# New engine orders, padded memory products and discarded products in a fused attention and dynamic-convolution kernel

## The chip, the cores and the metric

One NeuronCore of a Trainium2 chip runs the kernel. The metric is the device time in microseconds. Five instruction streams run side by side: TensorE (PE), VectorE (DVE), ScalarE (ACT), GpSimd (POOL) and SyncE (SP), which here only issues DMAs. Each executes its own list in order; they meet through semaphores.

## What is computed

The input is 16 images of 128 channels and 32 x 32 pixels, in float32. Two stages follow each other, each on a group norm of its input and each added to it.

```
x = x + attention(group_norm(x))       # linear attention, 4 heads of 32, 4 memory keys and values
x = x + dynamic_conv(group_norm(x))    # 3 x 3 convolution, filters mixed per image from 3 experts

# attention: q is normalised over the channels of a head, k over all pixels
xn = rmsnorm(x) * g1
q, k, v = w_qkv @ xn                    # k and v get 4 memory columns more
q = softmax(q, over channels) * scale;  k = softmax(k, over pixels)
context = k @ v.T;  out = context.T @ q
out = rmsnorm(w_out @ out + b_out) * g2

# dynamic convolution: a gate per expert and input channel, from 16 pooled cells
y = relu(rconv_w @ pooled(x) + rconv_b);  r = sigmoid(relu(fc_w @ y + fc_b))
w = sum over experts k of r[k, c] * expert_weight[k, o, c, :, :]
out = conv3x3(x, w)                     # padding 1
```

## The kernel before

One image has its channels on the 128 partitions and its 1024 pixels along the row. Eight tiles of 128 pixels each are turned on TensorE where pixels have to stand on the partitions.

The work is a software pipeline over images. In step `t` each engine works on several images at once: a part that is called with age `a` works on image `t - a`. `do(part, t, p, a)` issues a part for that image if there is one, `turn` does the same for the shared group statistics (of image `t` for the first norm and `t - 3` for the second), and `once` puts a part of the setup into one step. Steps run from -1 to 20. Those up to 8 and from 15 on are written out (unrolled), and those from 9 to 14 are three rounds of a loop of two steps. Nothing reorders the instructions: each engine has its own function `step(t, p)`, and the order of the lines in it is the order of its list.

The main parts, by engine and with the line of the profile:

- TensorE. The transposes of x (L1122) feed the sum of squares. Each of the eight `project` tiles has three products of rounded operands (L1135 to L1137). The transpose of the partial key maximum (L1143) and its spread over all partitions (`k_shift`, L1148) give the key maximum. `key_contexts` has one product with the 4 memory keys (L1154) and eight with the tiles (L1156). Then come the transposes of its result (L1161) and of q (`q_transpose`, L1179), `contexts` with the 4 memory values (L1166) and the rest (L1167), `mixes` (L1171), `outputs` (L1189) and the transposes of y (L1195). The group norms need two small products, the group means (L1110) and the group variances (L1115). `routing` (L1202) feeds the gates. The convolution has 54 products an image (L1225), 27 for each half of the image; `conv(n)` issues the next n of them, so they fill the list between the other parts. A plain float32 product is run as two passes, which the profile counts as two instructions. The convolution and the projections use operands split into a rounded part and a rest, in one pass a product.
- VectorE. The maxima over keys and queries, the subtractions and sums of the softmaxes, the statistics, the second residual (L900), the gates, the passes over the filters (L999, L1006, and L1012, which adds one to the centre tap), and the low part of the image (L936). `rms1` (L785) scales the eight sums of squares of an image; GpSimd raises them to the power -1/2 (L490).
- ScalarE. The exponentials, the squares, the high parts (`high1` L582, `filters_high` L659), the first pass over the filters (`w_first`, L653, which writes into the space of expert_raw), and the evacuations of PSUM (the projections' is L592, the result's L668).
- GpSimd. The low parts of x and of the filters (L483, L528), the scaling of q_exp (`q_normalise`, L501) and of x_nt (L495), the first norm (L476), the powers, and four small operations that zero the edge columns of the shifted images (`image_edges`, L535).
- SyncE. The loads of an image twice (`xa`, `xb`), the store, and four copies of the image shifted by one pixel.

The experts' filters are turned in nine groups of TensorE transposes during steps 0 to 2 (`expert_transpose`, L1094), through the PSUM buffers `ps_conv` of the convolution; ScalarE (L674) and VectorE (L989) evacuate them. The first convolution runs in step 4.

The memory tiles `memk_exp`, `memv_t` and `mem_ones` have 4 partitions, so the products L1154 and L1166 use 4 rows of the array:

```
mm(ps_att[:, 0:CEXT], memk_exp[:, :], mem_ones[:, :], start=True, stop=False)
mm(ps_att[:, 0:HID], memv_t[:, :], memk_exp[:, :], start=True, stop=False)
```

## Time and profile before

| | |
|---|---|
| median of 3 runs | 477.28 us (476.15 to 477.4) |
| the profiled execution | 476.64 us, span 474.9 us |
| TensorE busy, mean granted clock | 425.4 us (90%), 0.96 |
| VectorE busy | 373.1 us (79%) |
| ScalarE busy | 293.3 us (62%) |
| GpSimd busy | 253.3 us (53%) |
| HBM | 58 GB/s over the span |

The span is counted from the first to the last instruction. Busy time is the time in which at least one instruction of an engine runs. Matmuls are pipelined, so that a busy TensorE is not one at its peak: the distance from one start to the next says more than a duration does. A chain of waits is followed back from the last instruction, at each step to what released it; "issue" in it is time in which the engine waited for nothing that the profile shows.

### The profile page before, as it was taken

The numbers are of one execution on the slowest core, as the hardware profiler recorded it, in microseconds if no ns is written. First come the engines' busy times: TensorE is split into PE (matmuls) and PEld (weight loads), VectorE is DVE, ScalarE is ACT, GpSimd is POOL, SyncE is SP. The second block draws the span as 40 slices with busy tenths as digits, with TensorE's granted clock in tenths as the row PEclk, the third lists the DMA queues.
The fourth block names the chain that finished last, engine by engine and source line by source line (L and its number), as shares of the span: only waits on it lengthen the run. The fifth ranks groups of instructions, "written<-read, shape, count | busy, mean of one in ns | idle before, by whom it ended". The sixth has DMA issues, their size and how long they took to land.

```text
span 474.9 us, 8615 instructions
## 1 busy us (share of the span) xinstructions
PE 425.4 (90%) x2478; PEld 357.6 (75%) x2478; DVE 373.1 (79%) x773; ACT 293.3 (62%) x903; POOL 253.3 (53%) x247
## 2 busy tenths in 40 slices
PE   2868775999999999999999999999999999999796
PEld 1757674888778787878787787878788877868575
DVE  3374969798998979797979989797979797886720
ACT  2575676566676776766666667767666667554221
POOL 4635554648283747556482837575564838242220
PEclk9969595999999999999999999999999999999899
DMA  7320224224434160626243341605252332424331
GB/s 215 129 89 2 88 90 177 91 88 149 162 129 183 58 238 16 224 88 224 88 160 152 121 188 53 239 17 221 88 221 89 124 143 89 178 77 190 134 132 44
DMA packets 18786, 61.61 MB, mean 130 GB/s; under 512 B 2992, under 2 KB 4032, under 8 KB 18752
## 3 DMA queue, kind: packets, MB, share of 16 engines
q1 hardware_dynamic: 18752, 61.21, 34.1%
q8 instruction: 15, 0.25, 0.2%
q14 instruction: 19, 0.16, 0.1%
HBM read 19.29 MB, written 8.39 MB: 58 GB/s over the span
## 4 chain that ended last, share of the span: by engine, by line
PE 33%; DVE 31%; issue 23%; ACT 6%; DMA 3%; SPq 1%; DVEq 1%; POOL 1%; POOLq 0%; ACTq 0%
PE ps_conv L1225 7%; PE ps_y L1189 6%; DVE w_full L1006 4%; DVE stats L907 3%; DVE q_sum L848 3%; PE ps_y L1179 3%; DVE route_terms L954 3%; ACT expert_raw L653 3%; DVE k_half L792 2%; PE ps_att L1156 2%; DMA expert_raw<-_conv_expert_weight_dram 2%; DVE y_scaled L888 2%; ACT qk L592 2%; DVE x L900 2%; PE ps_qkv L1135 2%
## 5 line engine op out<-in xcount | busy, mean ns | idle before, releaser
L592 ACT ACTIVATE qk<-ps_qkv,scale 128x256 f32<-128x256 f32 x128 | 55.0, 468 | 13.8 <-PE ps_qkv L1137 13.8
L659 ACT ACTIVATE w_hi<-w_full 128x1152 fp32r<-128x1152 f32 x16 | 18.7, 1167 | 60.6 <-DVE w_full L1012 60.6
L528 POOL TENSOR_TENSOR w_lo<-w_full,w_hi 128x1152 fp32r<-128x1152 f32 x16 | 42.6, 2662 | 23.7 <-ACT w_hi L659 13.6
L509 POOL TENSOR_TENSOR scale<-ssq,minus_half 128x8 f32<-128x8 f32 x16 | 26.2, 1637 | 44.3 <-DVE ssq L881 44.3
L1135 PE MATMUL ps_qkv<-wqk_hi,x_hi 128*128 128x256 f32 x128 | 42.4, 331 | 3.7 <-ACT qk L592 3.7
L483 POOL TENSOR_TENSOR x_lo<-x,x_hi 128x1024 fp32r<-128x1024 f32 x16 | 38.2, 2387 | 12.8 <-ACT x_hi L582 12.8
L535 POOL TENSOR_TENSOR left_hi<-zeros 128x32 fp32r<-128x32 f32 x16 | 4.0, 250 | 75.0 <-DMA right_lo<-img_lo 75.0
L633 ACT ACTIVATE y_scaled<-ps_y 128x128 f32<-128x128 f32 x128 | 33.3, 291 | 12.7 <-PE ps_y L1189 12.7
L1225 PE MATMUL ps_conv<-left_hi,w_lo 128*128 128x512 f32 (+1 forms) x96 | 39.8, 414 | 0.0
L1225 PE MATMUL ps_conv<-img_hi,w_lo 128*128 128x512 f32 x96 | 39.7, 413 | 0.0
L1225 PE MATMUL ps_conv<-img_hi,w_hi 128*128 128x512 f32 x96 | 38.5, 401 | 1.1 <-POOL w_lo L528 1.1
L1225 PE MATMUL ps_conv<-right_lo,w_hi 128*128 128x512 f32 (+1 forms) x96 | 39.1, 408 | 0.0
L1225 PE MATMUL ps_conv<-right_hi,w_hi 128*128 128x512 f32 (+1 forms) x96 | 38.7, 403 | 0.0
L1225 PE MATMUL ps_conv<-img_lo,w_hi 128*128 128x512 f32 x96 | 38.5, 401 | 0.0
L1225 PE MATMUL ps_conv<-left_hi,w_hi 128*128 128x512 f32 (+1 forms) x96 | 37.8, 394 | 0.0
L1225 PE MATMUL ps_conv<-left_lo,w_hi 128*128 128x512 f32 (+1 forms) x96 | 37.8, 393 | 0.0
L1225 PE MATMUL ps_conv<-right_hi,w_lo 128*128 128x512 f32 (+1 forms) x96 | 37.6, 392 | 0.0
L1136 PE MATMUL ps_qkv<-wqk_lo,x_hi 128*128 128x256 f32 x128 | 36.9, 288 | 0.0
L1137 PE MATMUL ps_qkv<-wqk_hi,x_lo 128*128 128x256 f32 x128 | 36.8, 288 | 0.0
L1156 PE MATMUL ps_att<-x_nt,k_exp 128*128 128x130 f32 x256 | 36.1, 298 | 0.0
L1156 PEld LDWEIGHTS ps_att<-x_nt,k_exp 128*128 128x128 f32 x256 | 32.9, 207 | 2.2 <-issue 0.5
L565 ACT ACTIVATE squares<-ps_qkv 128x128 f32<-128x128 f32 x128 | 33.1, 275 | 1.5 <-PE ps_qkv L1122 1.5
(147 smaller groups left out, 1327.7 us busy)
## 6 DMA issues: line engine op xcount, KB each, us to landing
xa<-in_x_dram SPq DMA_DIRECT2D x16, 512.0 KB, 4.0
xb<-in_x_dram SPq DMA_DIRECT2D x16, 512.0 KB, 4.8
out_dram<-expert_raw SPq DMA_DIRECT2D x16, 512.0 KB, 2.9
left_hi<-img_hi SPq DMA_DIRECT2D x16, 511.5 KB, 2.9
right_hi<-img_hi SPq DMA_DIRECT2D x16, 511.5 KB, 3.7
left_lo<-img_lo SPq DMA_DIRECT2D x16, 511.5 KB, 2.9
right_lo<-img_lo SPq DMA_DIRECT2D x16, 511.5 KB, 3.7
expert_raw<-_conv_expert_weight_dram SPq DMA_DIRECT2D x1, 1728.0 KB, 8.6
```

Of the source, the lines that this page charges most:

```text
L483: nc.gpsimd.tensor_tensor(x1_lo[:, :], x1[:, :], x1_hi[:, :].bitcast(F32), ALU.subtract).then_inc(x1_lo_done, 1)
L509: nc.gpsimd.tensor_tensor(scale2[:, :], ssq2[:, :], minus_half[:, :], ALU.pow).then_inc(scale2_done, 1)
L528: nc.gpsimd.tensor_tensor(w_lo[p][:, :, :].rearrange("p t o -> p (t o)"), w_full[:, :], w_hi[p][:, :, :].bitcast(F32).rearrange("p t o -> ...
L565: last = nc.scalar.activation(squares[:, tile(t)], ps_qkv[h][:, tile(t % (NT // 2))], ACT.Square, accum_out=ssq1_sum[:, t:t + 1])
L592: nc.scalar.activation(qk[:, t, :], ps_qkv[t % 2][:, 0:QK], ACT.Copy, scale=scale1[:, t:t + 1]).then_inc(qkv_done, 1)
L633: last = nc.scalar.activation(y_scaled[:, t, :], ps_y[:, tile(t)], ACT.Square, accum_out=ssq2_sum[:, t:t + 1])
L1135: mm(o, x1_hi[:, tile(t)], wqk_hi[:, :], start=True, stop=False)
L1136: mm(o, x1_hi[:, tile(t)], wqk_lo[:, :], start=False, stop=False)
L1137: mm(o, x1_lo[:, tile(t)], wqk_hi[:, :], start=False, stop=True).then_inc(qkv_ps, 1)
L1156: last = mm(ps_att[:, 0:CEXT], k_exp[:, t, :], x_nt[p][:, t, :], start=False, stop=(t == NT - 1))
L1189: last = mm(ps_y[:, tile(t)], q_t[p][:, tile(t)], mix[p][:, :], start=True, stop=True)
L1225: last = mm(into, weight[:, tap, :], pixels[:, top + down:bottom + down, :], start=(n == 0), stop=(n == 3 * TAPS - 1))
```

## The change

It has three parts.

**Orders.** The order of the lines in `step` of TensorE, VectorE and ScalarE is new. GpSimd's list keeps its cyclic order and is only cut into steps at another place; SyncE's is the same. Ages that grow by one mean the same: on ScalarE and VectorE, too, the cut between two steps moves, and parts ahead of it are called with an age larger by one.

**Padding.** `memk_exp`, `memv_t` and `mem_ones` have 128 partitions. GpSimd sets the first two to zero at the start, and only their first 4 partitions are written afterwards, so that L1154 and L1166 have 128 rows and give the same sums.

**Discarded products.** `keep_busy` issues products of a tile of ones, 64 columns wide, into an unused part of `ps_stat`, at five places of steps 2 and 3 alone. Their results are never read.

```
-        memv_t = sb("memv_t", [MEM, HID])
-        mem_ones = sb("mem_ones", [MEM, CEXT])
+        memv_t = sb("memv_t", [128, HID])
+        mem_ones = sb("mem_ones", [128, CEXT])
-        memk_exp = sb("memk_exp", [MEM, HID])
+        memk_exp = sb("memk_exp", [128, HID])
+            nc.gpsimd.memset(memv_t[:, :], 0.0)
+            nc.gpsimd.memset(memk_exp[:, :], 0.0)
...
-                nc.scalar.activation(memk_exp[:, :], memk_exp[:, :], ACT.Exp).then_inc(memk_exp_done, 1)
+                nc.scalar.activation(memk_exp[0:MEM, :], memk_exp[0:MEM, :], ACT.Exp).then_inc(memk_exp_done, 1)
...
+            IDLE_PRODUCTS = {"key_contexts": {2: 8, 3: 6}, "project": {2: 6, 3: 6}, "k_part_transpose": {2: 5, 3: 9},
+                             "k_shift": {2: 4, 3: 4}, "y_transpose": {2: 2, 3: 3}}
+
+            def keep_busy(t, place):
+
+                if not isinstance(t, int) or t not in IDLE_PRODUCTS[place]:
+                    return
+                turns = t if place == "key_contexts" else t + 1
+                pe.wait_ge(gvar_done, turns)
+                if turns > GAP:
+                    pe.wait_ge(route_y_done, turns - GAP)
+                for _ in range(IDLE_PRODUCTS[place][t]):
+                    mm(ps_stat[:, 448:512], ones[:, :], ones[:, 0:64], start=True, stop=True)
...
+                once(expert_transpose, t, 0, 0)
+                do(x_transpose, t, p, 0, 0)
+                do(x_transpose, t, p, 0, 1)
+                keep_busy(t, "k_part_transpose")
                 do(k_part_transpose, t, p, 1)
...
                 do(y_transpose, t, p, 2)
-                conv(2)
-                once(expert_transpose, t, 0, 0)
+                conv(1)
```

The last piece also shows two moves of the first steps: the first group of expert transposes, which waits for the load of the experts, stands ahead of the transposes of the first image, where it stood behind them; and both halves of the transposes of x stand ahead of the transpose of the partial key maximum. The other eight expert groups, spread over steps 1 and 2, are spread over steps 1 to 3.

On ScalarE, `high1` (L582) moves from ahead of `filters_high` to behind the exponential of q, and the first half's result from behind `filters_high` to ahead of it.

VectorE, in a middle step, from the last pass over the gates to the residual of y (gate_n are the gates, k_max_part and k_max_all the partial and the full key maximum). Before:

```order
L936 SCALAR_TENSOR_TENSOR img_lo<-x_1,nmean,img_hi 128x1024
L999 SCALAR_TENSOR_TENSOR w_second<-experts,gate_n,expert_raw 128x1152
L792 TENSOR_TENSOR k_half<-qk 128x512
L798 TENSOR_TENSOR k_quarter<-k_half 128x256
L804 TENSOR_TENSOR k_max_part<-k_quarter 128x128
L1006 SCALAR_TENSOR_TENSOR w_full<-experts,gate_n,w_second 128x1152
L833 TENSOR_REDUCE q_max<-qk 128x32
L1012 TENSOR_TENSOR w_full<-w_full,ident 128x128
L811 TENSOR_REDUCE k_max<-ps_att 128x1
L840 TENSOR_TENSOR q_exp<-qk,q_max 128x1024
L818 TENSOR_SCALAR k_max_all<-k_max,memk_max 128x1
```

After (the lines of the changed kernel are a few higher):

```order
L938 SCALAR_TENSOR_TENSOR img_lo<-x_0,nmean,img_hi 128x1024
L748 BN_AGGR meanvar<-stats 128x2
L1001 SCALAR_TENSOR_TENSOR w_second<-experts,gate_n,expert_raw 128x1152
L794 TENSOR_TENSOR k_half<-qk 128x512
L1008 SCALAR_TENSOR_TENSOR w_full<-experts,gate_n,w_second 128x1152
L835 TENSOR_REDUCE q_max<-qk 128x32
L800 TENSOR_TENSOR k_quarter<-k_half 128x256
L1014 TENSOR_TENSOR w_full<-w_full,ident 128x128
L806 TENSOR_TENSOR k_max_part<-k_quarter 128x128
L842 TENSOR_TENSOR q_exp<-qk,q_max 128x1024
L813 TENSOR_REDUCE k_max<-ps_att 128x1
L820 TENSOR_SCALAR k_max_all<-k_max,memk_max 128x1
```

The partial maximum has moved behind the centre tap's addition, the full one with it, and the aggregate of the first norm has come in.

VectorE, the stretch that follows, from the sums of q to the group means (nmean). Before:

```order
L848 TENSOR_REDUCE q_sum<-q_exp 128x32
L854 RECIPROCAL q_rsum<-q_sum 128x32
L900 SCALAR_TENSOR_TENSOR x_1<-ps_y,g_c,xb 128x1024
L785 TENSOR_SCALAR ssq<-ssq_sum 128x8
L907 BN_STATS stats<-x_1 128x6 x2
L746 BN_AGGR meanvar<-stats 128x2
L915 BN_AGGR meanvar<-stats 128x2
L921 TENSOR_REDUCE pooled<-x_1 128x16
L757 TENSOR_SCALAR nmean<-ps_stat 128x2
```

After:

```order
L850 TENSOR_REDUCE q_sum<-q_exp 128x32
L856 RECIPROCAL q_rsum<-q_sum 128x32
L902 SCALAR_TENSOR_TENSOR x_1<-ps_y,g_c,xb 128x1024
L909 BN_STATS stats<-x_1 128x6 x2
L787 TENSOR_SCALAR ssq<-ssq_sum 128x8
L917 BN_AGGR meanvar<-stats 128x2
L923 TENSOR_REDUCE pooled<-x_1 128x16
L759 TENSOR_SCALAR nmean<-ps_stat 128x2
```

The scaling of the sums of squares (L785, now L787) has moved behind the statistics, and the first norm's aggregate is gone from here.

TensorE, from the key contexts to the contexts. Before:

```order
L1154 MATMUL ps_att<-mem_ones,memk_exp 128x130
L1156 MATMUL ps_att<-x_nt,k_exp 128x130 x8
L1225 MATMUL ps_conv<-left_hi,w_lo 128x480
...
L1225 MATMUL ps_conv<-img_hi,w_hi 128x480
L1225 MATMUL ps_conv<-img_lo,w_hi 128x480
L1110 MATMUL ps_stat<-meanvar,group_avg 128x2
L1161 MATMUL ps_att<-ident,k_x 128x128
L1179 MATMUL ps_y<-ident,q_exp 128x128 x8
L1166 MATMUL ps_att<-memk_exp,memv_t 128x128
```

After:

```order
L1156 MATMUL ps_att<-mem_ones,memk_exp 128x130
L1158 MATMUL ps_att<-x_nt,k_exp 128x130 x8
...
L1241 MATMUL ps_conv<-img_hi,w_hi 128x480
L1241 MATMUL ps_conv<-img_lo,w_hi 128x480
L1181 MATMUL ps_y<-ident,q_exp 128x128 x4
L1163 MATMUL ps_att<-ident,k_x 128x128
L1112 MATMUL ps_stat<-meanvar,group_avg 128x2
L1181 MATMUL ps_y<-ident,q_exp 128x128 x4
L1168 MATMUL ps_att<-memk_exp,memv_t 128x128
```

The group means (L1110, now L1112) have moved behind half of the transposes of q and the transpose of k_x.

## Rows read from the trace of the kernel before

**Rows 1.** The page: TensorE's granted clock in 40 slices of 11.9 us, in tenths.

```profile
PEclk9969595999999999999999999999999999999899
```

**Rows 2.** Busy time by stage: length, busy us and count per engine, PEclk, DMA.

```profile
34.00:56.00 22.00, 16.73 (x99) 14.94 (x98) 13.96 (x27) 13.76 (x54) 11.40 (x8) 0.73 0.15 54
56.00:79.00 23.00, 14.79 (x87) 13.37 (x87) 18.61 (x42) 14.12 (x41) 11.52 (x13) 0.72 0.36 138
131.00:157.00 26.00, 24.82 (x154) 21.00 (x153) 23.17 (x49) 18.04 (x57) 15.60 (x15) 1.00 0.38 143
```

**Rows 3.** The chain of waits, whole run: start us, us, what (passes).

```profile
56.41 3.77 PE ps_att L1156 x16
...
73.95 1.41 DVE w_full L1006
...
142.64 1.78 PE ps_y L1189 x16
...
212.61 2.00 PE ps_att L1156 x16
...
412.28 1.41 DVE w_full L1006
...
439.02 0.89 PE ps_y L1195 x8
...
458.51 12.52 PE ps_conv L1225 x54
```

**Rows 4.** VectorE's timeline, one step: start, us, instruction, [idle before, releaser].

```profile
125.80 1.41 DVE L1006 SCALAR_TENSOR_TENSOR w_full<-experts,gate_n,w_second 128x1152 f32<-128x1152 f32 x1
...
128.25 0.28 DVE L1012 TENSOR_TENSOR w_full<-w_full,ident 128x128 f32<-128x128 f32 x1
...
129.79 0.20 DVE L818 TENSOR_SCALAR k_max_all<-k_max,memk_max 128x1 f32<-128x1 f32 x1
...
135.02 1.77 DVE L785 TENSOR_SCALAR ssq<-ssq_sum 128x8 f32<-128x8 f32 x1
...
144.90 0.43 DVE L943 TENSOR_TENSOR route_y<-ps_stat,rconv_bias 128x256 f32<-128x256 f32 x1 [1.56 <-PE ps_stat L1202]
...
151.73 1.41 DVE L1006 SCALAR_TENSOR_TENSOR w_full<-experts,gate_n,w_second 128x1152 f32<-128x1152 f32 x1
```

**Rows 5.** TensorE's timeline, the same step.

```profile
134.00 0.48 PE L1154 MATMUL ps_att<-mem_ones,memk_exp 4*128 4x130 f32 x2
134.41 2.06 PE L1156 MATMUL ps_att<-x_nt,k_exp 128*128 128x130 f32 x16
...
138.47 0.35 PE L1110 MATMUL ps_stat<-meanvar,group_avg 128*128 128x2 f32 x2 [1.00 <-DVE meanvar L746]
```

**Rows 6.** The instructions of L785: shortest, median and longest duration in ns.

```profile
L785 DVE TENSOR_SCALAR ssq<-ssq_sum x16: 171/1782/1868, 14.9 to 395.6; 128x8 f32<-128x8 f32 x16
```

**Rows 7.** GpSimd's timeline, the same step as rows 4.

```profile
129.87 2.67 POOL L528 TENSOR_TENSOR w_lo<-w_full,w_hi 128x1152 fp32r<-128x1152 f32 x1 [1.22 <-issue]
...
134.84 1.93 POOL L501 TENSOR_TENSOR q_exp<-q_exp,q_rsum 128x1024 f32<-128x1024 f32 x1
```

**Rows 8.** ScalarE's timeline, the same step.

```profile
149.51 1.24 ACT L582 ACTIVATE x_hi<-xa,shift,rstd 128x1024 fp32r<-128x1024 f32 x1
```

**Rows 9.** TensorE's timeline, the first steps.

```profile
11.50 0.90 PE L1122 MATMUL ps_qkv<-ident,x 128*128 128x128 f32 x3 [1.88 <-DVE memk_max L729]
...
15.27 1.98 PE L1094 MATMUL ps_conv<-ident,expert_raw 128*128 128x128 f32 x8 [1.80 <-DMA expert_raw<-_conv_expert_weight_dram]
...
16.90 0.56 PE L1135 MATMUL ps_qkv<-wqk_hi,x_hi 128*128 128x256 f32 x1
...
33.72 0.77 PE L1154 MATMUL ps_att<-mem_ones,memk_exp 4*128 4x130 f32 x2 [0.93 <-issue]
```

**Rows 10.** The timelines of VectorE and of GpSimd at 51.7 us.

```profile
51.80 0.20 DVE L818 TENSOR_SCALAR k_max_all<-k_max,memk_max 128x1 f32<-128x1 f32 x1
...
51.74 2.36 POOL L483 TENSOR_TENSOR x_lo<-x,x_hi 128x1024 fp32r<-128x1024 f32 x1 [3.81 <-ACT x_hi L582]
```

More of the change, by code:

```diff
@@ L699, in step @@
                 do(qkv_evacuate, t, p, 1, 0)
+                once(expert_evacuate, t, 3, 8)
                 do(qkv_evacuate, t, p, 1, 1)
@@ L705, in step @@
                 do(squares2, t, p, 2)
-                do(gate_exponent, t, p, 3)
-                do(qkv_evacuate, t, p, 1, 4)
-                do(qkv_evacuate, t, p, 1, 5)
+                once(expert_evacuate, t, 1, 2)
             run_steps(act, step)
@@ L1021, in step @@
             def step(t, p):
+                do(q_subtract, t, p, 2)
+                do(k_maximum, t, p, 2)
+                do(k_maximum_all, t, p, 2)
+                do(y_scale, t, p, 3)
+                do(k_subtract, t, p, 2)
                 do(q_sums, t, p, 2)
@@ L1030, in step @@
                 turn(means, t, p, 0)
+                do(k_sums, t, p, 2)
                 turn(differences, t, p, 0)
@@ L1238, in conv @@
                         next(products, None)
-                once(expert_transpose, t, 1, 1)
-                conv(4)
-                once(expert_transpose, t, 2, 7)
                 conv(1)
+                once(expert_transpose, t, 2, 6)
+                conv(3)
+                once(expert_transpose, t, 3, 8)
+                conv(2)
+                keep_busy(t, "key_contexts")
                 do(key_contexts, t, p, 2)
-                conv(1)
                 do(project, t, p, 1, 0)
                 conv(2)
+                do(q_transpose, t, p, 2, 0)
+                do(key_context_transpose, t, p, 2)
                 turn(group_means, t, p, 0)
-                do(key_context_transpose, t, p, 2)
-                do(q_transpose, t, p, 2, 0)
                 do(q_transpose, t, p, 2, 1)
                 do(contexts, t, p, 2)
+                once(expert_transpose, t, 1, 1)
                 do(project, t, p, 1, 1)
+                conv(1)
                 turn(group_variances, t, p, 0)
+                do(mixes, t, p, 2)
+                do(project, t, p, 1, 2)
                 conv(1)
-                do(mixes, t, p, 2)
-                conv(1)
-                do(project, t, p, 1, 2)
-                do(project, t, p, 1, 3)
-                once(expert_transpose, t, 1, 2)
-                do(outputs, t, p, 2)
-                do(routing, t, p, 3)
-                do(project, t, p, 1, 4)
-                conv(4)
+                do(project, t, p, 1, 3)
+                do(outputs, t, p, 2)
+                once(expert_transpose, t, 1, 2)
+                do(routing, t, p, 3)
+                conv(4)
+                do(project, t, p, 1, 4)
+                once(constants, t, 0)
+                conv(1)
                 do(project, t, p, 1, 5)
-                conv(2)
+                conv(1)
                 once(expert_transpose, t, 1, 3)
-                conv(3)
+                conv(6)
+                keep_busy(t, "project")
                 do(project, t, p, 1, 6)
@@ L1271, in step @@
                 do(project, t, p, 1, 7)
-                conv(1)
+                conv(5)
                 once(expert_transpose, t, 1, 4)
                 once(expert_transpose, t, 1, 5)
-                conv(3)
-                once(expert_transpose, t, 1, 6)
-                conv(11)
-                do(k_part_transpose, t, p, 1)
-                conv(6)
-                once(expert_transpose, t, 2, 8)
-                conv(2)
-                once(constants, t, 0)
-                conv(4)
-                do(x_transpose, t, p, 0, 0)
-                conv(2)
+                conv(1)
+                once(expert_transpose, t, 2, 7)
+                conv(14)
+                once(expert_transpose, t, 0, 0)
+                do(x_transpose, t, p, 0, 0)
+                do(x_transpose, t, p, 0, 1)
+                keep_busy(t, "k_part_transpose")
+                do(k_part_transpose, t, p, 1)
+                conv(5)
+                keep_busy(t, "k_shift")
                 do(k_shift, t, p, 1)
-                conv(3)
-                do(x_transpose, t, p, 0, 1)
+                conv(5)
+                keep_busy(t, "y_transpose")
                 do(y_transpose, t, p, 2)
-                conv(2)
-                once(expert_transpose, t, 0, 0)
+                conv(1)
             run_steps(pe, step)
```

71 lines of the change are left out of this document (33 added, 38 removed).

## The prediction

> **What bounds the kernel now.** I read the windows by stage first, then the chain of waits over the whole run, then the chain and the timelines of one step. From 79 us on TensorE is granted its full clock; between 25 and 80 us it falls to half again and again [rows 1, 2]. A middle step holds 24.82 us of TensorE work and 23.17 of VectorE work in 26 us [rows 2], so neither engine is simply full. The chain shows what sets the step. The pass over the filters (L1006) comes 13 steps apart at 73.95 and 412.28: 26.02 us a step [rows 3]; in the undisturbed step that I follow, 25.93 [rows 4].
>
> I follow that step from the start of the centre tap's addition (L1012, "the centre", 128.25; the next one is at 154.18, being 2.45 behind its L1006) [rows 4]. VectorE works on until its group statistics are ready, TensorE stands still for 1.00 us at the group means (138.47) [rows 5] and then runs to the end of the outputs, 144.42 [rows 3]. VectorE, idle for 1.56 us, starts the routing sum (L943) at 144.90 [rows 4], and from there its chain reaches the next centre. Four links: 10.22 (centre to group means), 5.95 (to the end of the outputs), 0.48, and 9.28: 25.93 in all.
>
> Two things in it aren't work. L785, eight elements wide, takes 1.77 us at 135.02; its fastest case took 171 ns and its median 1782 [rows 4, 6]. It ends at 136.79, and GpSimd's scaling of q_exp runs from 134.84 to 136.77 [rows 7]: VectorE is held until GpSimd lets go. And the pair of passes with 4 rows (L1154) takes 0.41 us from its start to the next matmul, where passes of 128 rows go by at 0.11 (1.78 over 16) [rows 3, 5].
>
> **The change, part by part.** *VectorE's order.* L785 moves behind the two statistics of x2, 1.2 us later. GpSimd's scaling ended 8.52 behind the centre; L785 now comes at 8.25 and waits some 0.3 instead of 1.6. The aggregate of the first norm leaves the place ahead of the second norm's (0.26). So VectorE has both group statistics ready at 8.85 behind the centre instead of 10.1.
>
> TensorE doesn't get there by then, so its own order is late next. The maximum over all keys (L818) stood 1.54 behind the centre [rows 4]; the partial maximum is now put between (0.21, and 0.07 for a result that is waited for): 1.82. Its product starts 0.26 later, as before: 2.08. Behind that stand 14 convolution products at 0.232 (12.52 over 54) [rows 3], 3.25 us; 33 passes at 0.111, 3.66; three projection products, 0.36; and three changes back from plain to rounded operands, 0.08 each. That is 7.5, so the group means come at 9.6 instead of 10.22: **0.65 saved**.
>
> *Between group means and outputs.* Four of the eight transposes of q (0.44) and the transpose of k_x (0.11) now lie ahead of the group means, and the 4-row pair of the contexts is padded (0.20 of its 0.41): 5.20 instead of 5.95, **0.75 saved**.
>
> *From the routing to the centre.* w_second waits for w_first as before. The partial maximum (0.21) moves past the centre, with 0.07 of waiting for a result; the aggregate that moved in lies in the wait for w_first: 9.0 instead of 9.28, **0.28 saved**. The new step is 9.6 + 5.2 + 0.48 + 9.0 = 24.25 us.
>
> *TensorE's own length* is the floor: 54 products at 0.232 (12.5), 24 projections at 0.12 (2.9), 74 passes at 0.111 (8.2) and seven changes at 0.08 (0.6): 24.2. Loop and floor meet, so small hitches no longer vanish in slack. One I can name: GpSimd's four edge operations, which fell under a reduction with one input, now fall under the quarter maximum, the centre and the partial maximum, all with two inputs from SBUF. Their price lies between 0 and 1.0 (four of 0.25), and I take 0.1 to 0.2. I put the step at 24.4, and with the 0.09 by which the mean of all steps exceeded the quiet one, 24.45: 1.57 less, 13 times, **20.4 us**. The bounds: 24.2 (24) and 25.4 (8).
>
> *The padding itself.* Two more memsets on GpSimd before its constants: 0.3 us, hidden, since the first use of them waits for the first image's statistics. A padded pass streams as many columns as before. By the row, the pairs get shorter by 0.2 each, twice a step.
>
> *ScalarE's order.* x1_hi moves behind the exponential of q. q's exponential can start at 1.6 behind the centre, as before, and takes about a microsecond (an estimate from x1_hi's 1.24 for as many elements [rows 8]); x1_hi then ends at 3.9. GpSimd can use it at 4.3, when w_lo (2.67 from 129.87 [rows 7]) is over: free in the loop, 0.4 from mattering. The exponential of k then ends at 6.1 to 6.2, where TensorE reaches the key contexts at 6.1: between 0 and 0.3, inside the 0.2 above. The first half's result now fills the wait ahead of w_hi. GpSimd's and SP's orders in the loop stay.
>
> *The first steps.* TensorE's first expert transposes now stand ahead of the first image's transposes. Those ran at 11.50, the experts' at 15.27 when their DMA had landed, and the first projection at 16.90 [rows 9]. Now the image waits for the experts: transposes at 16.1, squares and copies 3.7 behind, projection at 19.9, **3 us lost**. Part comes back, and I take it for half: the partial maximum's transpose stood behind an expert group that waited for its evacuation, and no longer does. In step 2 x1_hi costs up to 2 us, since nothing covers it: the key contexts start near 35.8 instead of 33.72 [rows 9].
>
> Against that stands the clock. Steps 2 and 3 ran at 0.73 and 0.72 of full [rows 2]. Sixteen passes of the key contexts took 3.77 us in step 3 and take 2.00 at full clock [rows 3]; the transposes beside them lose in proportion. The discarded products are 53, two passes each, and at twice the 0.111 of a pass, 0.22 a pair, they need 11.7 us. Their groups are of 0.4 to 2.0 us; TensorE is idle there for a third of the two steps' 45 us (16.73 + 14.79 busy [rows 2]), once for 0.93 just ahead of the key contexts [rows 9]: most fit. If the clock holds from the middle of step 2, about 1 us comes back there and 2.8 by the group means and transposes of step 3. Balance: **2 us gained**; bounds, 3 gained and 4 lost (clock as before, some groups longer than their waits, at 0.28 a pair on the low clock).
>
> *The tail.* The last full step (TensorE's work without a break up to the transposes at 439.02) loses its wait and its slow pairs: **1.5 us**. From 439.02 to the last 54 products at 458.51 a single image's chain runs [rows 3]; of it nothing is removed.
>
> The sum: 20.4 + 2 + 1.5 = 24. The profiled execution took 476.64 for a span of 474.9; 476.64 − 24 gives **452.6 us**. The median shown is 477.28, 0.6 above that execution.
>
> **The rivals.** *A. The wait moves on.* L785 still waits for GpSimd, the edge operations cost their full price, and ScalarE's key exponential comes late: a step of 25.2 to 25.4. For it: in three places (L785, the key contexts, the partial maximum's transpose) two engines now meet within 0.3 us. Against: at the group means VectorE has 0.75 to spare. Time: 476.64 − 13 × 0.7 − 3, some 464.
>
> *B. VectorE is locked out at L818, and the kernel gets slower.* L818 used to be issued 0.08 before GpSimd's w_lo (129.79 and 129.87) [rows 4, 7]. With the partial maximum ahead of it, it comes at 1.82 behind the centre, after w_lo has begun at 1.62. If it is held as L785 was, it waits until w_lo ends, 2.67 later at 4.29; everything behind it comes 2.47 later, and the step is 26.7. Then 13 × 0.7 is lost, 3.5 gained in the early steps and the tail: 482 us. The point from which it decides is a wait of 1.7 at L818. Against it: at 51.80 L818 started 0.06 after GpSimd had begun x_lo (51.74, 2.36 long) and took its usual 0.20 [rows 10]. It is one case, and of one element where L785 has eight. The Trainium skill ("SBUF — State Buffer", Who interferes with whom) tells of a port pair that VectorE and GpSimd share under an exclusive lock: a VectorE instruction in a two-port mode, or with two SBUF inputs, is blocked until a GpSimd instruction that began first is over. L785's row agrees with it, the row at 51.80 does not extend it to a single element; if it held there too, the time would be this rival's.
>
> *C. The loop gains as worked out, but the beginning loses.* The late experts and x1_hi cost their full price and the discarded products bring no clock: 4 lost instead of 2 gained, 458.6 us. For it: TensorE only has transposes and waits between 26 and 33, and the first group of products starts on the low clock.
>
> **How the numbers follow.** The forecast has 0.62, A 0.2, C 0.11, B 0.06, and 0.01 is for a change that moves nothing. The forecast's own range is 448 to 458. To leave out no more than 2 in 10, the range takes in C and most of A: 446 to 465. A difference of 0.3% (1.4 us) is about what can be told from none. Only B is slower, only a chance meeting of A and C with worse prices gives no change: faster 0.92, same 0.02, slower 0.06.
>
> **What would show it.** Right: L1006's new line every 24.3 to 24.6 us; L785 at 0.2 to 0.7; no wait of TensorE at the group means; the key contexts' opening pair at half its time; the first projection near 19.9; full clock from about 37. Wrong: L818's line longer than 0.3 (B); steps of 25 with waits before the outputs or the key contexts (A); a first filter pass later than 74 (C).

## The result and the profile after

| | before | after |
|---|---|---|
| median | 476.71 us (474.76 to 477.4, 4 runs) | 459.72 us (456.25 to 461.23, 4 runs) |
| ratio, 95% interval | | 0.964 [0.9576, 0.9703] |
| profiled execution, span | 476.64, 474.9 us | 460.37, 458.6 us |
| TensorE, VectorE, GpSimd busy | 425.4, 373.1, 253.3 us | 425.5, 357.0, 265.4 us |

The kernel is faster, inside the range, by 16.3 us of span in the profiled execution where I had forecast 24; its four runs spread over 5 us. The loop gave more than I had worked out; the first steps took 6 us where I had them give 2; the tail gave nothing.

**The loop.** The chain of waits of the changed kernel (start us, us, what). Every line number of the vector engine is two higher than before.

```profile
6.60 8.89 DMA expert_raw<-_conv_expert_weight_dram
15.63 1.10 PE ps_conv L1096 x4
...
105.46 1.41 DVE w_full L1008
...
395.68 1.41 DVE w_full L1008
...
422.62 0.89 PE ps_y L1197 x8
...
442.26 12.52 PE ps_conv L1241 x54
```

From 105.46 to 395.68 there are twelve steps: 24.19 us each, against 26.02 [rows 3]. The two rows at the top, with an end of their own, come back below. VectorE's timeline of one middle step, for [rows 4]:

```profile
180.67 0.29 DVE L1014 TENSOR_TENSOR w_full<-w_full,ident 128x128 f32<-128x128 f32 x1
...
182.53 0.21 DVE L820 TENSOR_SCALAR k_max_all<-k_max,memk_max 128x1 f32<-128x1 f32 x1
...
189.08 0.59 DVE L787 TENSOR_SCALAR ssq<-ssq_sum 128x8 f32<-128x8 f32 x1
189.58 0.20 DVE L917 BATCH_NORM_AGGREGATE meanvar<-stats 128x2 f32<-128x12 f32 x1
...
191.22 0.81 DVE L772 SCALAR_TENSOR_TENSOR spread<-dev,meanvar 128x1 f32<-128x1 f32 x2
...
195.97 0.42 DVE L945 TENSOR_TENSOR route_y<-ps_stat,rconv_bias 128x256 f32<-128x256 f32 x1 [1.01 <-PE ps_stat L1204]
```

TensorE's timeline of that step, for [rows 5]:

```profile
186.93 0.38 PE L1156 MATMUL ps_att<-mem_ones,memk_exp 128*128 128x130 f32 x2
187.15 1.95 PE L1158 MATMUL ps_att<-x_nt,k_exp 128*128 128x130 f32 x16
188.86 0.36 PE L1137 MATMUL ps_qkv<-wqk_hi,x_hi 128*128 128x256 f32 x1
...
190.29 0.28 PE L1112 MATMUL ps_stat<-meanvar,group_avg 128*128 128x2 f32 x2
190.44 0.63 PE L1181 MATMUL ps_y<-ident,q_exp 128*128 128x128 f32 x4
190.91 0.41 PE L1168 MATMUL ps_att<-memk_exp,memv_t 128*128 128x128 f32 x2
191.15 0.39 PE L1169 MATMUL ps_att<-x_k,wqkv_t 128*128 128x128 f32 x2
...
195.34 0.60 PE L1204 MATMUL ps_stat<-route_prod,rstd 128*128 128x256 f32 x2
```

The four links again. Centre to group means: 190.29 − 180.67 = 9.62 (9.6 predicted), and no idle time stands behind L1112. Group means to routing, which starts as the outputs end: 5.05, where it was 5.79 on the same timeline (144.26 − 138.47). To route_y 0.63. From there to the next centre, at 204.93, 8.96 (9.0 predicted). In all 24.26 us, and the stage table of this step shows no time in which TensorE stands:

```profile
180.67:204.93 24.26, 24.26 (x155) 21.09 (x154) 21.77 (x49) 18.11 (x56) 17.14 (x14) 1.00 0.41 153
```

The line of L787 alone, and of the full maximum, for [rows 6] (shortest, median, longest in ns):

```profile
L787 DVE TENSOR_SCALAR ssq<-ssq_sum x16: 153/182/1223, 19.8 to 382.7; 128x8 f32<-128x8 f32 x16
```

```profile
L820 DVE TENSOR_SCALAR k_max_all<-k_max,memk_max x16: 212/214/215, 34.0 to 400.4; 128x1 f32<-128x1 f32 x16
```

The first has lost its wait (median 1782 before), the second never got one: rival B did not come. In 7 of its 16 cases w_lo had begun before it (by 0.27 us at 110.22, for one).

**The first steps.** The granted clock in 40 slices, and the two stages of [rows 2]:

```profile
PEclk9995997699999999999999999999999999999899
```

```profile
34.00:56.00 22.00, 20.62 (x133) 20.00 (x133) 10.34 (x21) 13.56 (x51) 11.36 (x8) 0.77 0.14 49
56.00:79.00 23.00, 19.58 (x146) 18.47 (x146) 20.86 (x46) 15.69 (x54) 12.03 (x9) 0.91 0.36 138
```

The mean clock of both stages is higher (0.77 and 0.91, where 0.73 and 0.72 stood) and TensorE is busier, and still everything is later. TensorE's timeline, for [rows 9]:

```profile
15.63 1.10 PE L1096 MATMUL ps_conv<-ident,expert_raw 128*128 128x128 f32 x4 [5.82 <-DMA expert_raw<-_conv_expert_weight_dram]
16.52 1.92 PE L1124 MATMUL ps_qkv<-ident,x 128*128 128x128 f32 x8
20.43 0.55 PE L1137 MATMUL ps_qkv<-wqk_hi,x_hi 128*128 128x256 f32 x1 [1.99 <-ACT x_nt L575]
...
39.05 0.75 PE L1156 MATMUL ps_att<-mem_ones,memk_exp 128*128 128x130 f32 x2
39.59 3.67 PE L1158 MATMUL ps_att<-x_nt,k_exp 128*128 128x130 f32 x16
...
77.28 3.94 PE L1220 MATMUL ps_stat<-ones 128*128 128x64 f32 x18
...
95.50 0.38 PE L1117 MATMUL ps_stat<-spread,group_avg 128*128 128x2 f32 x2 [1.67 <-DVE spread L772]
```

The first projection is at 20.43 instead of 16.90, the key contexts of step 2 at 39.05 instead of 33.72, and on the low clock as before (3.67 for sixteen passes). The discarded products of step 3 (77.28) also ran on the low clock, 0.22 a pass. The centre of the first image is at 79.55 (76.41 before), that of the second at 108.28 (102.32). So 6.0 us are lost up to there, 22.2 are won by twelve steps (108.28 to 398.47, where 102.32 to 414.73 stood), and from the centre of the fourteenth image to the end it takes 60.1 us as before: the 16.3 (all of the two profiled executions).

### The profile page after: what moved, and what is told of

Read it like the earlier page. It is cut to its first block, busy times and chain, and to the rows that moved or that the text cites. A ratio compares the mean times of both kernels' runs of the same rounds, so it can differ in the third digit from the quotient of the medians.

```text
span 458.6 us, 8839 instructions
## 1 busy us (share of the span) xinstructions
PE 425.5 (93%) x2584; PEld 372.4 (81%) x2584; DVE 357.0 (78%) x773; ACT 295.1 (64%) x903; POOL 265.4 (58%) x249
## 4 chain that ended last, share of the span: by engine, by line
PE 57%; DVE 15%; issue 11%; ACT 8%; DMA 4%; POOL 2%; SPq 1%; DVEq 0%; ACTq 0%; POOLq 0%
PE ps_conv L1241 22%; PE ps_y L1191 6%; PE ps_att L1158 5%; DVE w_full L1008 3%; ACT expert_raw L655 3%; PE ps_y L1181 2%; PE ps_stat L1220 2%; DMA xa<-in_x_dram 2%; PE ps_qkv L1137 2%; PE ps_y L1197 2%; PE ps_qkv L1139 2%; PE ps_qkv L1138 2%; DMA expert_raw<-_conv_expert_weight_dram 2%; DVE route_terms L956 2%; ACT qk L594 2%
## 5 line engine op out<-in xcount | busy, mean ns | idle before, releaser
L594 ACT ACTIVATE qk<-ps_qkv,scale 128x256 f32<-128x256 f32 x128 | 56.4, 471 | 10.5 <-PE ps_qkv L1139 7.9
L537 POOL TENSOR_TENSOR left_hi<-zeros 128x32 fp32r<-128x32 f32 x16 | 7.6, 476 | 82.1 <-DMA right_lo<-img_lo 82.1
L1241 PE MATMUL ps_conv<-right_lo,w_hi 128*128 128x512 f32 (+1 forms) x96 | 42.0, 437 | 0.0
L1241 PE MATMUL ps_conv<-img_hi,w_hi 128*128 128x512 f32 x96 | 39.6, 412 | 1.9 <-POOL w_lo L530 1.6
L1241 PE MATMUL ps_conv<-right_hi,w_lo 128*128 128x512 f32 (+1 forms) x96 | 38.7, 403 | 0.0
L1241 PE MATMUL ps_conv<-img_hi,w_lo 128*128 128x512 f32 x96 | 37.7, 392 | 0.0
L1241 PE MATMUL ps_conv<-left_hi,w_lo 128*128 128x512 f32 (+1 forms) x96 | 37.6, 392 | 0.0
L670 ACT ACTIVATE expert_raw<-ps_conv,gmean 128x512 f32<-128x512 f32 x32 | 21.7, 678 | 24.7 <-PE ps_conv L1241 24.7
L1158 PE MATMUL ps_att<-x_nt,k_exp 128*128 128x130 f32 x256 | 33.0, 284 | 0.0
```

The lines of the kernel that those rows point to most:

```text
L594: nc.scalar.activation(qk[:, t, :], ps_qkv[t % 2][:, 0:QK], ACT.Copy, scale=scale1[:, t:t + 1]).then_inc(qkv_done, 1)
L1158: last = mm(ps_att[:, 0:CEXT], k_exp[:, t, :], x_nt[p][:, t, :], start=False, stop=(t == NT - 1))
L1241: last = mm(into, weight[:, tap, :], pixels[:, top + down:bottom + down, :], start=(n == 0), stop=(n == 3 * TAPS - 1))
```

## The experiments

Ratios are to the kernel before. "Centres" are the starts of the addition to the centre tap, from the profiled execution; the mean step is from the second to the fourteenth (before 26.03, after 24.18).

The first steps differ from one execution to the next even where the instructions up to there are the same, as they are in e2, e7, e8 and e9 up to the second image's transposes. TensorE's first products are 0.21 us apart in all of them; they change to 0.12 at 18.5 us in e2, 19.4 in e7 and 18.9 in e9, but only at 25.0 in e8, and the second image's transposes start at 23.39, 23.86, 23.45 and 25.60. (e10, e11 and e12, with small edits ahead of them, are like e8: the change at 24.0 to 24.9.) So some 2 us of a difference between two first centres can be this alone, and what an edit of the first steps is worth is read from the ratios.

| | ratio, 95% | first, second centre | mean step |
|---|---|---|---|
| the changed kernel | 0.9640 [0.9576, 0.9703] | 79.55, 108.28 | 24.18 |
| e1, no discarded products | 0.9633 [0.9596, 0.9670] | 79.71, 106.07 | 24.23 |
| e2, image first | 0.9521 [0.9494, 0.9548] | 71.89, 99.69 | 24.15 |
| e3, full maximum 8 wide | 1.0038 [1.0009, 1.0068] | 77.63, 105.22 | 25.87 |
| e4, before with L785 moved | 0.9747 [0.9718, 0.9776] | 76.96, 102.27 | 24.90 |
| e5, before with padding | 0.9874 [0.9855, 0.9892] | 73.40, 98.92 | 25.76 |
| e6, changed, not padded | 0.9779 [0.9760, 0.9799] | 79.95, 108.12 | 24.69 |
| e7, e2 and no discards | 0.9544 [0.9521, 0.9566] | 74.64, 101.18 | 24.15 |
| e8, e2 and x1_hi early | 0.9674 [0.9650, 0.9697] | 81.15, 110.75 | 24.19 |
| e9, e2, discards moved | 0.9412 [0.9392, 0.9433] | 68.98, 96.79 | 24.31 |
| e10, e9 and spreads first | 0.9395 [0.9371, 0.9419] | 71.18, 95.67 | 24.27 |
| e11, e2, two products | 0.9488 [0.9452, 0.9524] | 73.82, 103.77 | 23.93 |
| e12, e2, scaling moved back | 0.9742 [0.9706, 0.9777] | 74.60, 102.29 | 25.09 |

**e1, without the discarded products.**

```
-            IDLE_PRODUCTS = {"key_contexts": {2: 8, 3: 6}, "project": {2: 6, 3: 6}, ...
+            IDLE_PRODUCTS = {"key_contexts": {}, "project": {}, "k_part_transpose": {}, ...
```

> The changed kernel without any discarded product; orders and padding stay. In the changed kernel the discards of step 3 ran on the low clock (18 passes in 3.7 us from 77.28) and the transpose of the partial key maximum came 1.0 us after its input was ready, the spread of the maximum 0.8 and the transposes of y 1.4. Theory 1, the discards cost more than they bring: the first centre (the centre tap's addition) comes within 0.5 us of 79.55, the step from the first to the second centre shrinks from 28.7 to about 26, the steady step stays at 24.2, and the whole is 1.5 to 3 us faster (ratio to before 0.958 to 0.961 against 0.964). Theory 2, the discards keep the clock up in steps 2 and 3 and pay for themselves: the granted clock from 44 to 74 us falls from 1.00 to 0.7, the first centre comes 1.5 to 3 us later, and the whole is 1 to 3 us slower (0.966 to 0.970).

The same time within what can be told (0.3 us by the ratios, give or take 3.5). The clock does fall more often:

```profile
PEclk9997877799999999999999999999999999999999
```

but the first centre is where it was and the second 2.2 us earlier. As placed, the discarded products bring nothing that shows: they hold the clock up from 44 to 74 us (1.00, in e1 0.83), where TensorE still waits for other engines (26.55 us busy of 30). In step 3 18 of their passes take 3.94 us, and from the first to the second centre it takes 28.73 us, in e1 26.36.

**e2, the first image's transposes ahead of the experts'.**

```
-                once(expert_transpose, t, 0, 0)
                 do(x_transpose, t, p, 0, 0)
                 do(x_transpose, t, p, 0, 1)
+                once(expert_transpose, t, 0, 0)
```

> The changed kernel with the first image's transposes ahead of the first expert transposes in step 0, as before the change. Theory 1 (the expert load holds the first image): the first projection starts at 16.9 to 17.2 instead of 20.43, and all that follows comes 2.5 to 3.5 us earlier, the first centre at 76 to 77; ratio 0.957 to 0.959. Theory 2 (something later in steps 1 and 2 sets the pace, as the evacuations of the experts did): the first projection comes earlier but the first centre by less than 1 us; ratio within 0.002 of 0.964.

5.7 us by the ratios, with an interval of 2.4 to 9.0, and 7.7 at the first centre. The same edit between e1 and e7, both without discarded products, gives 4.2 (2.2 to 6.3) and 5.1 at the first centre. The 3 that I had priced lies inside both, at their lower end. TensorE in e2:

```profile
16.11 0.56 PE L1137 MATMUL ps_qkv<-wqk_hi,x_hi 128*128 128x256 f32 x1
...
25.81 0.33 PE L1145 MATMUL ps_att<-ident,k_max_part 128*128 128x128 f32 x1 [1.36 <-DVE k_max_part L806]
27.40 0.49 PE L1150 MATMUL ps_att<-ident,k_max_all 128*128 128x128 f32 x2 [1.26 <-DVE k_max_all L820]
...
28.18 3.01 PE L1220 MATMUL ps_stat<-ones 128*128 128x64 f32 x16
31.36 0.77 PE L1156 MATMUL ps_att<-mem_ones,memk_exp 128*128 128x130 f32 x2 [0.17 <-issue]
31.93 3.67 PE L1158 MATMUL ps_att<-x_nt,k_exp 128*128 128x130 f32 x16
```

Of the 7.7, 4.3 is the first projection itself (16.11 against 20.43; 3.4 between e1 and e7). The rest comes in step 1: TensorE runs that step's projections and transposes of the changed kernel at 0.21 a product (24.66, 24.87, 25.09), the distance of its low-clock stretch at 43 us, where e2 has 0.12; the clock's own row shows 1.00 there, so that the distance alone tells it. From the first projection to the next transposes of x it takes 10.06 us (to 30.49), in e2 7.28 (to 23.39). But this isn't shown to be the order's doing. TensorE had stood 5.82 us for the DMA; yet e8, e10, e11 and e12, with the image first and waits of 1.7 to 2.1 there, have the 0.21 until 24 us too, and e8 takes 9.62 for the same stretch. The two rows that open the changed kernel's chain say it too: the load of the experts has become the start of the whole chain.

**e3, the full maximum over 8 elements.** Only its first column is used.

```
-        k_max_all = sb("k_max_all", [128, 1])
+        k_max_all = sb("k_max_all", [128, 8])
```

> The changed kernel with the full key maximum (L820) taken over 8 elements instead of 1; the other 7 are a constant that nothing reads, so the output is the same. Theory 1, a single-input VectorE instruction from SBUF to SBUF is held by a running GpSimd instruction only when it has several elements: L820 takes its 0.21 us where GpSimd is idle or in its edge operations and up to 2.7 us where w_lo has begun; since w_lo now begins just behind L820 (182.74 against 182.53), the race may be won: then nothing moves. Where it is lost a step costs 1 to 2.5 us more. Theory 2, the kind of instruction does not matter but the moment: L820 stays at 0.21 and the time within 0.3% of the changed kernel's.

All of the gain is gone. VectorE in e3:

```profile
185.25 2.43 DVE L821 TENSOR_SCALAR k_max_all<-k_max,memk_max 128x8 f32<-128x8 f32 x1
```

GpSimd in e3:

```profile
185.01 2.63 POOL L531 TENSOR_TENSOR w_lo<-w_full,w_hi 128x1152 fp32r<-128x1152 f32 x1 [1.07 <-ACT w_hi L662]
```

It begins 0.24 behind w_lo, ends with it (187.68 and 187.64), and TensorE stands for 2.24 ahead of the key shift. In eight of sixteen images it took 2.28 to 2.46 us, in the others 0.23 to 0.29. So rival B's mechanism is real, to the 2.47 us that I had given it, and the kernel escapes it by the width of one operand: a single element was never held in 16 cases of the changed kernel, though w_lo had begun before it in 7 of them; and in e3 the eight that were held are just those before which w_lo had begun. The Trainium skill ("SBUF — State Buffer", Who interferes with whom) tells of an exclusive lock on a shared port pair; the eight elements agree with it, and that one element goes free is what these rows add.

**e4, the kernel before with L785 alone moved.**

```
-                do(rms1, t, p, 1)
                 do(gn2_stats, t, p, 3)
+                do(rms1, t, p, 1)
```

> The kernel before with one line moved: L785 (the scaling of the eight sums of squares) stands behind the two statistics of x2 instead of ahead of them, on VectorE alone. Theory 1, L785 was held by GpSimd's scaling of q_exp and this is on the chain: L785 falls from 1.77 to 0.2 to 0.5 us, TensorE's 1.0 us wait at the group means shrinks to below 0.2, and the step falls from 25.93 to 24.8 to 25.1, so that the whole gains 11 to 15 us (ratio 0.969 to 0.977). Theory 2, the two engines' other orders must move together: the wait turns up elsewhere (the scaling of q_exp, the variances), the step stays above 25.6 and the ratio above 0.99.

One line gives 2.5 of the changed kernel's 3.6%, 1.13 us a step of the 1.85.

**e5, the kernel before with the padding alone.** **e6, the changed kernel without it.** Each is the padding part of the diff above, or its undoing.

> The kernel before with the padding alone. The prediction's theory: each pair of the memory products gets 0.2 us shorter; the one ahead of the contexts lies in full on the stretch from the group means to the outputs, the one ahead of the key contexts lies in front of the convolution's products, behind which TensorE waits 1.00 for the group means anyway. So 0.2 us a step over 13 steps and as much in the first steps and the tail: some 3 us, ratio about 0.994, steps of 25.8 instead of 26.0. Rival: the pair's length is the change between arrays of 4 and 128 rows and is hidden by waits, ratio 0.998 to 1.002. Second rival: 128 rows cost more than they save (zeros are streamed all the same), ratio over 1.002.

> The changed kernel with the memory tiles of 4 partitions again. In it TensorE works without a wait in most of a step, so both pairs should count: 0.2 to 0.4 us a step, steps of 24.4 to 24.6 instead of 24.18, 3 to 5 us in all, ratio 0.970 to 0.975 against the kernel before (the changed kernel had 0.964). Rival: VectorE's chain sets the step just as closely and hides a pair, ratio 0.963 to 0.967.

More than worked out in both: 0.27 a step in e5, 0.51 in e6, 1.4% of the time there. TensorE in e6:

```profile
188.34 0.48 PE L1154 MATMUL ps_att<-mem_ones,memk_exp 4*128 4x130 f32 x2
188.75 2.06 PE L1156 MATMUL ps_att<-x_nt,k_exp 128*128 128x130 f32 x16
190.56 0.36 PE L1135 MATMUL ps_qkv<-wqk_hi,x_hi 128*128 128x256 f32 x1
...
192.13 0.64 PE L1179 MATMUL ps_y<-ident,q_exp 128*128 128x128 f32 x4
192.69 0.48 PE L1166 MATMUL ps_att<-memk_exp,memv_t 4*128 4x128 f32 x2
193.11 0.49 PE L1167 MATMUL ps_att<-x_k,wqkv_t 128*128 128x128 f32 x2
193.35 0.36 PE L1135 MATMUL ps_qkv<-wqk_hi,x_hi 128*128 128x256 f32 x1
```

The 4-row pair takes 0.42 to the next product where the padded one takes 0.24. But the product behind it is slower too: 0.24 (193.11 to 193.35) against 0.14, sixteen passes 1.81 against 1.71; and the pair starts 0.56 behind the four transposes instead of 0.47. The change of shape is paid at both ends; I had read only the pair's own distance. e4 and e5 come to 1.40 of the 1.85 us a step, e12 and e6 to 1.45: some 0.4 is left for all other moves of the orders together, and no run takes these apart. In e5 another 3 us came at the first centre (73.40 against 76.41). 1.0 of them is there at the second image's transposes (27.46 against 28.45), ahead of the first padded product (32.69), so that no padded product can have brought it; the rest I have not isolated. The granted clock between 20 and 40 us was 0.96 and 0.70 in e5, 0.85 and 0.63 before.

**e7, e2 without the discarded products.** Both edits above.

> The changed kernel with the first image's transposes ahead of the experts' and without the discarded products. If the discarded products are worth nothing, it is as the version with the image first: ratio 0.950 to 0.954, the first addition to the centre tap near 72, the next near 98. If they cost where the clock stays low in spite of them (step 3: 18 passes of 0.2), 1 to 2 us less: 0.947 to 0.949. If they are worth something once the image comes first: 0.955 or more, and the first addition later than 73.

Not told apart from e2 with certainty: the intervals overlap, the medians are 454.39 and 453.34; the first centre is 2.8 us later, the second 1.5.

**e8, e2 with x1_hi ahead of filters_high in steps 2 and 3.**

```
+                if early:
+                    do(high1, t, p, 1)
                 do(filters_high, t, p, 4)
                 do(q_exponent, t, p, 2)
-                do(high1, t, p, 1)
+                if not early:
+                    do(high1, t, p, 1)
```

> The changed kernel with the first image's transposes ahead of the experts' and with x1_hi ahead of the filters' high parts in steps 2 and 3, as in the kernel before. If x1_hi behind the exponential of q delays the key contexts of these steps by up to 2 us each (the prediction's price), the first addition to the centre tap comes 1 to 3 us before 71.9 and the ratio is 0.945 to 0.950. If the steps are set by other work (the projections' evacuations, the low clock), nothing: 0.950 to 0.954.

Neither: 7.3 us slower, 9.3 at the first centre, of which 2.2 were there before the edit acts (the second image's transposes at 25.60 against 23.39). An early x1_hi releases GpSimd's low part early, and that begins just ahead of VectorE's partial maximum. GpSimd in e8:

```profile
52.00 2.64 POOL L485 TENSOR_TENSOR x_lo<-x,x_hi 128x1024 fp32r<-128x1024 f32 x1 [1.73 <-ACT x_hi L584]
```

VectorE in e8:

```profile
52.48 2.31 DVE L810 TENSOR_TENSOR k_max_part<-k_quarter 128x128 f32<-128x128 f32 x1
```

In e2 the same operation took 0.29 (at 48.45), as did the one before it (2.31 at 27.68 in e8, beside an x_lo that the edit starts at 27.39; 0.29 at 25.46 in e2). The move that I had charged with up to 2 us is in this order of VectorE a gain of some 7. The two holds are 4.0 of them; how the rest comes about isn't isolated.

**e9, the discarded products where the clock still falls.** On top of e2:

```
-"key_contexts": {2: 8, 3: 6}, ..., "k_part_transpose": {2: 5, 3: 9}, "k_shift": {2: 4, 3: 4}
+"key_contexts": {2: 12, 3: 6}, ..., "x_transpose": {3: 7}, "k_part_transpose": {1: 5, 2: 5, 3: 14}, "k_shift": {1: 5, 2: 5, 3: 5}
```

> The changed kernel with the first image's transposes ahead of the experts', and the discarded products put where TensorE's clock still falls in that version: five pairs behind the second image's transposes of step 1 and five ahead of its key maximum's spread, twelve instead of eight ahead of the key contexts of step 2, seven ahead of the transposes of x in step 3 and fourteen instead of nine behind them. If the clock holds, the key contexts of step 2 take 2.0 instead of 3.67 us and step 3 loses nothing to the low clock between 69.5 and 79.5 (some 2.5 us): the first addition to the centre tap near 70, the second 26 later, 3 to 4 us less than with the image first alone, ratio 0.943 to 0.946. If discarded products don't bring the clock back or hold it, or if other engines set these steps: 0.950 to 0.954 as there. If they are in the way: over 0.955.

The stage 60 to 80 us and the stage 30 to 40 us, in e2:

```profile
30.00:40.00 10.00, 9.10 (x55) 8.65 (x54) 4.68 (x11) 5.79 (x21) 7.58 (x6) 0.72 0.29 107
...
60.00:80.00 20.00, 17.39 (x102) 16.32 (x101) 18.42 (x35) 13.88 (x48) 11.79 (x12) 0.74 0.40 158
```

The same in e9:

```profile
30.00:40.00 10.00, 9.60 (x84) 9.40 (x83) 4.83 (x13) 7.28 (x29) 8.99 (x7) 1.00 0.30 107
...
60.00:80.00 20.00, 18.17 (x146) 16.79 (x145) 19.13 (x39) 13.05 (x45) 11.99 (x11) 1.00 0.39 147
```

and TensorE's timeline in e9:

```profile
24.35 1.23 PE L1220 MATMUL ps_stat<-ones 128*128 128x64 f32 x10
25.87 0.33 PE L1145 MATMUL ps_att<-ident,k_max_part 128*128 128x128 f32 x1 [0.29 <-DVE k_max_part L806]
26.03 1.23 PE L1220 MATMUL ps_stat<-ones 128*128 128x64 f32 x10
...
31.73 1.95 PE L1158 MATMUL ps_att<-x_nt,k_exp 128*128 128x130 f32 x16
...
82.39 0.38 PE L1117 MATMUL ps_stat<-spread,group_avg 128*128 128x2 f32 x2 [1.81 <-DVE spread L772]
```

The granted clock is 1.00 from 20 to 83 us and the sixteen passes take 1.95 instead of 3.67; behind the wait of 1.81 at 82.39 it falls once (0.50 from 84 to 87). Discarded products that fill the waits before the clock falls (1.36 and 1.26 us of step 1) come, with the others that e9 adds, to 1.3% against e7, some 6 us (5 to 8), and 5.2 against e2; the first ones of the change came after the fall. e9 changes five groups at once, and no run tells which of them pays. Against e2, 1.8 us are gained by the first projection of step 2 (33.43 against 35.25) and 4.7 by that of step 4 (77.33 against 82.01). Its mean step is longer only for two steps of 25.04 and 25.18. 448.53 us is below both kernels.

**e10, e9 with VectorE's spreads ahead of the centring of the pooled cells.**

```
+                turn(spreads, t, p, 0)
                 do(gn2_centre, t, p, 3)
-                turn(spreads, t, p, 0)
```

> The version with the discarded products placed early, and on VectorE the two spreads of the group statistics ahead of the centring of the pooled cells. Behind it, the second spread meets GpSimd's multiplication of the routing products, which the centring releases, and its scaling of x_nt: the pair took 0.81 us in middle steps and 2.32 in step 4, where TensorE waited 1.81 for it. If the order is what makes them meet, the pair takes 0.34 everywhere, the 1.81 goes, and the middle steps stay at TensorE's 24.15: 1.5 to 2 us less than 448.5, ratio 0.936 to 0.939. If the routing, which now starts 0.3 later, is what ends last in that step, nothing: 0.940 to 0.943.

The pair of spreads takes 0.35 in every step, the wait of 1.81 at 82.39 is gone and with it the fall of the clock behind it, and the second centre is 1.1 us earlier though the first is 2.2 later. The medians, 447.73 and 448.53, differ by less than their intervals: the mechanism is shown, its worth in time is not.

**e11, e2 with two products in each projection tile.**

```
-                mm(o, x1_hi[:, tile(t)], wqk_lo[:, :], start=False, stop=False)
-                mm(o, x1_lo[:, tile(t)], wqk_hi[:, :], start=False, stop=True).then_inc(qkv_ps, 1)
+                mm(o, x1_hi[:, tile(t)], wqk_lo[:, :], start=False, stop=True).then_inc(qkv_ps, 1)
```

> The changed kernel with the first image's transposes ahead of the experts', and with two instead of three products in each tile of the projections (the one of the image's low part is left out, so q and k are less exact). It asks whether TensorE's length or VectorE's chain sets the step of 24.15 us. If TensorE is the floor, all eight products of 0.12 us count: steps of 23.2. If the chain does, only those between the centre and the end of the outputs count, four of 0.12: 23.7. If VectorE's chain alone is already as long, 24.1. Per cent against the kernel before: 0.925, 0.938 and 0.951.

With 0.96 us of TensorE's work gone the step shrinks by 0.22, to 23.93, and TensorE waits 0.42 for the partial maximum (at 176.28). TensorE's length is the floor of the changed kernel, and VectorE's chain lies 0.2 us beneath it. In time 1.6 us against e2 can't be told from none: its first steps came out late (second centre at 103.77 against 99.69), and whether by the edit or as those of e8, e10 and e12 did, no run tells.

**e12, e2 with the scaling back ahead of the statistics.** e4's edit the other way round.

> The changed kernel with the first image's transposes ahead of the experts', and with the scaling of the sums of squares back ahead of the two statistics, as in the kernel before. It is held by GpSimd's scaling again (about 1.5 us). The prediction's count gives VectorE 0.75 us to spare at the group means, so that 0.5 to 0.9 us a step would be lost: steps of 24.7 to 25.0, ratio 0.966 to 0.974. If what follows on VectorE (the second norm, the routing) is just as late as the group means, the whole wait comes back: steps of 25.3 or more, ratio 0.98 or more. If TensorE hides it all: 24.15 and 0.952.

0.94 a step in the profile, 2.2% in time, at the upper end of the theory's 0.5 to 0.9; where GpSimd had let go in time (steps of 24.21 and 24.31, L787 0.24 in both) next to nothing is lost.

## Why the prediction was right and where it was wrong

Right in sign and range. The forecast's 452.6 was 7 us too low, and its own narrower range, 448 to 458, was missed; what happened is nearest to rival C (the loop gains, the beginning loses: 458.6), to which I had given 0.11. Its mark, a first filter pass later than 74, is met: 76.76.

- **L785 behind the statistics.** Right: its median went from 1782 to 182 ns, and e4 and e12 show that the line alone gives most of the gain. VectorE has both statistics ready 9.1 behind the centre (8.85 predicted), since GpSimd let go at 8.97 and not at 8.52: w_lo began 2.07 behind the centre, as the edge operations were held (2.04 us for one at 180.35).
- **TensorE's links.** 9.62, 5.05, 0.63 and 8.96 against 9.6, 5.2, 0.48 and 9.0. The sum is right to 0.02 in this step (my third link ran from the end of the outputs, the one here from the start of the routing); the mean step, 24.18, was 0.27 below my 24.45, since the hitches that I added did not show. The floor of 24.2 was right (e11).
- **The padding.** The step "from the pair's own distance, 0.20" was too small for a pair: 0.27 a step in e5 and 0.51 in e6, as the products behind it pay as well.
- **The loop in sum.** 20.4 forecast; twelve steps gave 22.2. The thirteenth interval, from the first centre to the second, lost 2.8 and belongs to the first steps.
- **The first steps**, the term that failed: 2 gained forecast, 6.0 lost. The discarded products were to bring back 3.8; as placed they bring nothing that shows (e1, e7 against e2: 0.3 and 1.1 us, both within their intervals), since the clock was low before they start (35.74) and is at full only from 44 us, where I had put 37; the key contexts of step 2 took 3.67. Nor did I have a row for a pair on the low clock: I took 0.28 us, and 18 passes in 3.94 are 0.44 a pair. The order of the experts was priced at 3, half of it to come back; it cost 4.2 to 5.7 (e7, e2). Its shift of the first projection is 3.4 to 4.3, nothing is seen to come back, and whether the order also costs clock in step 1 stays open. x1_hi was charged with up to 2; its old place would have cost 7 (e8), so this term had the wrong sign, and made up for part of the other two.
- **The tail.** 1.5 forecast, nothing measured. The last full step has no projections, TensorE reached its group means without waiting for VectorE even before (423.35, no idle time), and there was no wait to remove: from the fourteenth centre to the fifteenth it took 21.71 us before and 21.41 after, and from there to the sixteenth 17.30 and 17.69. I had carried over a middle step's wait without a look at that row.
- **Rivals.** A did not come: L787 takes 0.15 to 0.80 us in a middle step (0.59 at 189.08, 0.80 at 140.81), so it is held for up to 0.65, which VectorE has to spare, and TensorE is without idle time in the step shown. B did not, by one element (e3): its condition, w_lo ahead of the full maximum, was met 7 times, and a single element isn't held.

## What to carry to other kernels

Before a small VectorE operation is moved, see which GpSimd instruction will have begun when it comes: one of eight elements can cost that instruction's whole rest, in every step in which they meet (e3: 8 of 16), and a new order earns most where it ends such meetings. Work that only keeps TensorE's clock up belongs in the waits ahead of the fall (e9); where it came behind it, it brought nothing (e1, e7). And work that waits for a late load is not put ahead of work that is ready: e2 gives 5.7 us for taking it back. Last, the first steps of one program can differ by 2 us between executions; a single profile doesn't price a move there.

## What the runs showed of the hardware

- VectorE operations on one element per partition with a scalar operator (L820) were never held by GpSimd (212 to 215 ns in 16 cases, 7 of them with w_lo begun first); the same on eight elements was held up to 2.46 us. But one element does not always save: the spreads (L772, one element, three operands from SBUF) took up to 1.93 us in the changed kernel.
- The hold works both ways: GpSimd's edge operations of 32 elements took 251 ns at the median and up to 2102 under VectorE's operations with two inputs.
- A pair of float32 passes with 4 rows between products of 128 costs at three places (e6, at 192.69): 0.1 us ahead of it, 0.18 in it, 0.1 behind it.
- In e2 TensorE idled for 1.36 and 1.26 us (ahead of 25.81 and 27.40), and its granted clock went from 1.00 to 0.50, the 1.2 GHz level, at 29 us, with discarded products already running; with products in those waits (e9) it stayed at 1.00, the 2.4 GHz level, until 83 us.
- The row of the granted clock can miss a low stretch at the start: in e8 it shows 1.00 from 19 to 24 us, while the projections' products are 0.21 apart as in low stretches (0.12 at full clock).
